# Linear attention and FFN on one core: x's turn ahead of the reciprocal, x1's turn behind it, and a new order of the transfers

## The reference

```
q, k, v = heads(x @ Wq.T + bq), heads(x @ Wk.T + bk), heads(x @ Wv.T + bv)
q, k = exp(q), exp(k)
kv  = cumsum(k[..., :, None] * v[..., None, :], axis=1)     # over the sequence
k1  = cumsum(k, axis=1)
num = einsum('zsD,zsDd->zsd', q, kv)
den = sum(q * k1, axis=-1)
x = layernorm(x + merge(num / den) @ Wo.T + bo)
h = x @ weight @ aux_weight1 @ aux_weight2
x = layernorm(x + tanh(h + bias))
```

## Time and profile before

| | |
|---|---|
| median of 3 runs | 2467.8 us (2459.77 to 2468.61) |
| profiled execution, its own time | 2467.03 us |
| span of its trace | 2465.3 us |
| PE busy | 2321.6 us, 94% |
| DVE busy | 1797.8 us, 73% |
| POOL busy | 1314.3 us, 53% |
| ACT busy | 1052.8 us, 43% |
| mean granted TensorE clock | 0.992 of full speed |

### The profile page before, as it was taken

How to read it: one execution, slowest core, us unless ns; L and a number is a source line. 1 busy time by engine, 2 the same in 40 slices (tenths; PEclk the granted TensorE clock), 3 DMA queues, 4 the chain that set the end, 5 groups by cost and what they waited for, 6 DMA issues and landing times.

```text
span 2465.3 us, 58596 instructions
## 1 busy us (share of the span) xinstructions
PE 2321.6 (94%) x21040; PEld 1907.9 (77%) x21040; DVE 1797.8 (73%) x2710; ACT 1052.8 (43%) x2039; POOL 1314.3 (53%) x1669
## 2 busy tenths in 40 slices
PE   6999999999999999999999999999999999999985
PEld 5778878877877887777777877777777877777764
DVE  4677777777777777777777777777777777777664
ACT  3434444444444444444444444444444444444431
POOL 1455555555655555555555555554555555555553
PEclk9999999999999999999999999999999999999998
DMA  6233333333333333333333333333333333333211
GB/s 162 71 98 103 106 99 102 103 98 96 105 100 100 103 100 97 104 98 99 102 97 100 102 99 100 102 99 99 99 101 100 100 102 99 98 103 96 64 65 52
DMA packets 293918, 241.90 MB, mean 98 GB/s; under 512 B 32848, under 2 KB 225360, under 8 KB 293712
## 3 DMA queue, kind: packets, MB, share of 16 engines
q1 hardware_dynamic: 293712, 238.69, 30.9%
HBM read 139.99 MB, written 98.57 MB: 97 GB/s over the span
## 4 chain that ended last, share of the span: by engine, by line
PE 93%; issue 4%; DVE 1%; ACT 1%; DMA 0%; SPq 0%; POOL 0%; POOLq 0%; ACTq 0%; DVEq 0%
PE G L310 25%; PE G L312 24%; PE G L311 24%; PE SC L377 6%; PE G L389 5%; PE G L364 4%; PE G L410 2%; PE G L401 1%; PE G L411 1%; PE SC L310 0%; PE SC L312 0%; PE SC L311 0%; DMA QT<-wqT 0%; DVE o L656 0%; SPq L272 0%
## 5 line engine op out<-in xcount | busy, mean ns | idle before, releaser
L775 POOL TENSOR_TENSOR qk1L<-WK,qk1H 128x512 fp32r<-128x512 f32 x128 | 165.4, 1292 | 814.7 <-ACT qk1H L555 814.7
L679 DVE RECIPROCAL o<-G 128x512 f32<-128x512 f32 x128 | 424.9, 3320 | 2.8 <-PE G L411 1.4
L673 DVE STREAM_TRANSPOSE SC<-WK 128x512 f32<-128x512 f32 x128 | 93.0, 727 | 448.5 <-DMA WK<-x_rows 448.5
L753 POOL TENSOR_SCALAR_AFFINE_SELECT A<-A 128x512 f32<-128x512 f32 x512 | 314.4, 639 | 10.7 <-issue 6.6
L517 ACT ACTIVATE A<-SC 128x512 f32<-128x512 f32 x512 | 275.3, 591 | 61.1 <-PE G L389 59.7
L792 POOL TENSOR_TENSOR xTL<-xin,xTH 128x512 fp32r<-128x512 f32 x128 | 164.8, 1288 | 245.6 <-ACT xTH L568 245.5
L310 PE MATMUL G<-WfH,x1H 128*128 128x512 f32 x512 | 211.1, 412 | 83.4 <-issue 71.7
L555 ACT ACTIVATE qk1H<-WK 128x512 fp32r<-128x512 f32 x128 | 81.0, 633 | 469.6 <-DVE WK L707 469.6
L724 DVE TENSOR_SCALAR WK<-xres,mv,rstd 128x512 f32<-128x512 f32 x128 | 200.5, 1566 | 86.4 <-POOL rstd L782 86.4
L533 ACT ACTIVATE x1H<-SC 128x512 fp32r<-128x512 f32 x128 | 76.6, 599 | 374.0 <-DVE SC L673 374.0
L310 PE MATMUL G<-xTH,WqH 128*128 128x512 f32 x512 | 203.0, 396 | 28.7 <-POOL xTL L792 21.1
(11 more groups left out here) (107 smaller groups left out, 5597.2 us busy)
## 6 DMA issues: line engine op xcount, KB each, us to landing
xin<-x SPq DMA_DIRECT2D x512, 64.0 KB, 1.9
xres<-x SPq DMA_DIRECT2D x128, 256.0 KB, 3.3
x_rows<-WK SPq DMA_DIRECT2D x128, 256.0 KB, 2.1
WK<-x_rows SPq DMA_DIRECT2D x512, 64.0 KB, 2.0
out<-WK SPq DMA_DIRECT2D x128, 256.0 KB, 2.1
k_rows<-WK SPq DMA_DIRECT2D x120, 256.0 KB, 2.3
WK<-k_rows SPq DMA_DIRECT2D x480, 64.0 KB, 2.0
QT<-wqT SPq DMA_DIRECT2D x4, 256.0 KB, 4.2
```

The costliest lines, as they stand in the source:

```text
L679: nc.vector.reciprocal(oflat, den_ps[:, :]).then_inc(recip_ready, 1)
L753: last = nc.gpsimd.affine_select(out=A[:, j, :, :], in_=A[:, j, :, :], compare_op=ALU.is_ge, fill=0.0, base=0, pattern=[[0, NK], [1, P]], ...
L775: nc.gpsimd.tensor_tensor(qk1L[:, :], WK[:, 7, :], qk1H[:, :].bitcast(F32), ALU.subtract).then_inc(qk1l_ready, 1)
```

## The change

VectorE: x's turn of tile k+8 moves from behind L724 to behind K's turn; the reciprocal follows it; x1's turn moves behind the reciprocal; the finished tile moves ahead of x1L. Queue: K's store and reads move ahead of the store of the finished tile; the load of the residual moves behind x1's reads and gets a wait for x1_ready, which is met by then. No operation and no transfer is added or taken away.

```diff
 queue, slot(c, k):
-                if c.exists(k - 3):
-                    n = k - 3
-                    wait_before(sp, (out_ready, c.count(n + 1)))
-                    sp.dma_start(out_t[n % B, c.it + n // B], y[:, n % 2, :]).then_inc(out_stored[n % B], 16)
                 if c.updates_state(k):
                     wait_before(sp, (k_turned, c.count(k + 1)))
                     sp.dma_start(k_rows, KS).then_inc(k_stored[k % B], 16)
...
+                if c.exists(k - 3):
+                    n = k - 3
+                    wait_before(sp, (out_ready, c.count(n + 1)))
+                    sp.dma_start(out_t[n % B, c.it + n // B], y[:, n % 2, :]).then_inc(out_stored[n % B], 16)
                 n = k - 1
                 if c.exists(n):
                     wait_before(sp, (x1_ready, c.count(k)))
                     sp.dma_start(x1_rows, x1[:, n % 2, :]).then_inc(x1_stored[n % B], 16)
-                if c.exists(k + 1):
...
-                    m = k + 1
-                    sp.dma_start(xres[:, m % 2, :], x_t[m % B, c.it + m // B]).then_inc(xres_loaded[m % B], 16)
                 if c.exists(n):
                     wait_before(sp, (x1_stored[n % B], c.dma_count(n)), (x1_turned, c.count(n)))
...
+                if c.exists(k + 1):
...
+                    wait_before(sp, (x1_ready, c.count(k)))
+                    m = k + 1
+                    sp.dma_start(xres[:, m % 2, :], x_t[m % B, c.it + m // B]).then_inc(xres_loaded[m % B], 16)

 VectorE, slot(c, k), behind K's turn:
-                if ffn:
-                    (x1's turn: wait for x1s_loaded and scores_out[0], transpose into x1T_ps)
+                if c.exists(k + 8):
+                    m = k + 8
+                    wait(dve, xin_loaded[m % B], c.part_count(m))
+                    xblocks = xin[:, m % XIN, :]
+                    nc.vector.transpose(xblocks, xblocks).then_inc(x_turned, 1)
                 if att:
                     (the reciprocal, unchanged)
                 if ffn:
-                    (x1L)
+                    (x1's turn)
                 if fin:
                     (the finished tile, unchanged)
+                if ffn:
+                    (x1L)
...
-                if c.exists(k + 8):
-                    (x's turn, behind L724)
```

More of the change, by code:

```diff
@@ L288, in slot @@
                     sp.dma_start(x1_rows, x1[:, n % 2, :]).then_inc(x1_stored[n % B], 16)
-                if c.exists(k + 1):
-                    if c.static() and c.it * B + k == -1:
-                        sp.wait_ge(c_done, 1)
-                    m = k + 1
-                    sp.dma_start(xres[:, m % 2, :], x_t[m % B, c.it + m // B]).then_inc(xres_loaded[m % B], 16)
                 if c.exists(n):
@@ L298, in slot @@
                                      x1_blocks[j]).then_inc(x1s_loaded[n % B], 16)
+                if c.exists(k + 1):
+                    if c.static() and c.it * B + k == -1:
+                        sp.wait_ge(c_done, 1)
+                    wait_before(sp, (x1_ready, c.count(k)))
+                    m = k + 1
+                    sp.dma_start(xres[:, m % 2, :], x_t[m % B, c.it + m // B]).then_inc(xres_loaded[m % B], 16)
             run_slots(sp, slot, 8, 3, {-7: load_wq_and_biases, -5: load_wk, -4: load_ffn_weights_and_wv,
@@ L667, in slot @@
                                         ).then_inc(k_turned, 1)
+                if c.exists(k + 8):
[3 more added lines that the diff above has]
+                    nc.vector.transpose(xblocks, xblocks).then_inc(x_turned, 1)
+                if att:
+                    wait(dve, den_done, c.count(k + 1))
+                    wait(dve, oh_ready, c.count(k))
+                    wait(dve, ol_ready, c.count(k))
+                    nc.vector.reciprocal(oflat, den_ps[:, :]).then_inc(recip_ready, 1)
                 if ffn:
@@ L674, in slot @@
                                         x1s[:, :].rearrange("p (t g f) -> p g t f", t=HG, f=HD)).then_inc(x1_turned, 1)
[L675 to L679, removed]
+                if fin:
+                    wait(dve, rstd2_ready, c.count(k - 2))
+                    nc.vector.tensor_scalar(yf, yf, mv2[:, 0:1], rstd[:, 1:2],
+                                            ALU.subtract, ALU.mult).then_inc(out_ready, 1)
                 if ffn:
@@ L684, in slot @@
                                             ALU.subtract).then_inc(x1l_ready, 1)
[L685 to L688, removed]
                 n = k + 1
```

## The result

The changed kernel takes 2907.8 us (median of 4 runs, 2901.0 to 2909.8) against 2464.6 for the kernel before: ratio 1.179, 95% interval [1.176, 1.183]. It is 443 us slower. The forecast was 2827, with a range of 2630 to 2960. One of the five executions of e3 took 4612.6 us and is left out of its figures.

A forecast was written before the change was run, and what follows sets the result against it. The prediction took x1's ring (18.51 us a slot) to bound the kernel, just above TensorE's 17.9. A new ring through x's load makes the slot 21.65: 2467 + 370 - 10 = 2827 us, range 2630 to 2960.

The forecast's parts named there:

- the ring of x1: x1's store, reads, turn and VectorE's operations to L724, once per slot: 18.51 us before, 14.5 us alone after the change.
- costs nothing: The reciprocal (3.24 us), ahead of x1's turn, fits VectorE's 4.27 us of idleness, so is free for x1's ring.
- The ring through x's load: New ring: VectorE awaits x's load, queued behind x1's store and reads, which await L724; 22.15 us a slot.
- Its queue part: From L724's end to x's turn: first x load issued after 4.81 us, 9.2 in all, bounds 8.09 and 10.8.
- Its VectorE part: VectorE from x's turn to L724's end: 0.70 + 3.24 + 9.01 = 12.95 us a slot.
- The term that was too small: The slot was forecast at 21.65 us, with no term for VectorE waiting on ScalarE's exponential of K.
- The tail: Last eight slots, no x awaited and reciprocal off x1's ring: between 0 and -23 us, -10 taken.
- the start: The kernel's first slots, which have no x1 ring: 0 us.
- The rule on the shared ports: VectorE's L724 beside GpSimd's L786: first issuer holds the ports, L724 takes 0.55 us; the forecast kept the row's 1.61.
- The rule on the clock: An idle TensorE is throttled; by the page the clock would fall in each slot with the idle stretch.
- The rival built on it: FFN product at 1.2 GHz in every slot and L724 long: 23.0 us a slot, +529, 2986 us; chance 0.08.
- The rival of the other side: x's load lands in time, slot falls to TensorE's 17.9 us below 4.9 us: 2386 us; chance 0.03.

The follow-up runs named there:

- e3: The kernel before with only the queue's new order, VectorE as before: 2447.2 us, ratio 0.992 to before.
- e7: The kernel before with VectorE's new order but x's turn not moved, and the queue as before: 2442.5 us, ratio 0.992.
- e5: The changed kernel with x's load early in the queue and ScalarE's exponential of K ahead of its four state copies: 2351.4 us, ratio 0.953 to before.
- e1: The changed kernel with x's turn put back behind L724, all else as changed: 2442.5 us, ratio 0.990 to before.
- e2: The kernel before with only x's turn moved, ahead of x1's turn and the reciprocal; queue as before: 2736.9 us, ratio 1.110.
- e4: The changed kernel with x's load moved in the queue ahead of the previous slot's x1 store, VectorE as changed: 2368.1 us, ratio 0.960 to before.
- e9: The changed kernel with x's load issued later, behind K's store and reads: 3494.7 us, 587 more than the changed kernel.
- e6: The changed kernel with ScalarE's exponential of K ahead of its four state copies: 2874.7 us, 33 us less than the changed kernel.
- e13: The changed kernel with 12 added matmuls of constants ahead of the FFN product, result unread: 2906.3 us, ratio 1.180 to before.

## Why the prediction was right

**The bound now** was read rightly in kind. Of two limits close together the ring of x1 decides: taking the reciprocal off it (e7) gave 0.8%, and with the waits for transfers off VectorE's way (e5) TensorE has hardly any idle time left. Two sizes were off. TensorE's own work is 17.6 us a slot (e5), not the 17.9 got by taking its idle time from the slot, so the limits stood 0.9 us apart. And the reciprocal's move alone was to win the 0.6 us of idle a slot; e7 won 0.17 (18.34 against 18.51), because the reciprocal, now early, waits for oL, 226.6 us in 112 slots. The prediction's "costs nothing" had left that wait out.

**The ring through x's load** was the mechanism. e1, e2, e4 and e9 tell it apart from everything else in the change: taken away two ways the loss is gone (2442.5, 2368.1), alone it makes 2736.9, and made longer by 5.56 us it makes each slot 4.97 longer.

**Its queue part** was forecast as 4.81 us to the first x load and 9.2 to x's turn. The sum came true (9.23 on the mean), but there is luck in it, since its two parts were off by half a microsecond each way. The trip shown has 4.75 us to the first x load; the mean over the slots is 5.35 (4.5 to 7.5), 0.54 more than forecast. The sum had been made of one undisturbed trip, and in the mean x1's store to its first read is 2.29 us instead of 2.16, the four reads 1.97 instead of 1.74, and the residual's load to x's 0.80 instead of 0.60, because now and then one issue takes over 1 us. The kernel before would have told: there the same transfers, in another order, take 5.35 us on the mean too. From the first x load to x's turn it is then 3.88 us, where 9.2 less 4.81 had left 4.39.

**Its VectorE part** was 12.95, with -0.5 for L724's operation. A slot in which nothing is waited for but rstd and L730 is long has 12.91 us (0.63 + 3.25 + 1.34 + 0.61 + 7.08), and L730 takes 1.08 us on the mean against 1.61, since it is long in one slot and short in the next: both are borne out. The waits below raise it again: 12.91 - 0.53 + 0.43 + 0.52 - 0.33 = 13.0, and 12.98 is measured.

**The term that was too small** is what I put at nothing: the slot is 21.65 + 0.56. 0.43 of it is VectorE's wait for ScalarE's exponential of K. At every fourth slot the scans begin a new group of four tiles and need the KT that ScalarE has just made; with x1's turn moved back behind the reciprocal, ScalarE's x1H, the exponential of Q, the four copies and the exponential of K all come later against VectorE, and the scans wait 1.7 us. I had followed x1H and stopped there. It is 50.4 us, and e6 got 33 back. It comes with VectorE's new order: e1 and e7 have it too (44.4 and 48.7 us, 28 slots each, from 160 to 2200 us), and the kernel before and e2 do not. The rest, 0.13, is about the FFN's lateness (61.0 us, 0.52 a slot) less what the wait for rstd gives back (79.9 us before, 41.4 after, 0.33 a slot).

**The tail** was to give 10 us and gave 2.4, and the start cost 3.4 where I had 0. With the 433 of the slots against 370 this is the 74 us between 2827 and the profiled execution's 2901.0.

**The rule on the shared ports.** I went by the row (1.61 us) against "Who interferes with whom" of the Trainium skill's SBUF — State Buffer. The trace after agrees with the row. L787, GpSimd's addition, never starts ahead of L730 there. In 64 of the 128 slots it starts 0.05 to 0.07 us behind it, and L730 takes 1.6 us. In the other 64 it starts 0.19 us or more behind it, in all but three after L730's end, and L730 takes 0.55. The page's rule, that the first to issue has the ports, fits those three and not the 64. Why it does not hold at so small a distance no run here shows.

**The rule on the clock.** The Trainium skill, TensorE: Matmul & The Clock Gate, "What's actually happening", has the idle array throttled. The trace agrees that the clock falls while TensorE stands still (0.50 from 1311 us on), but not that it would in each such slot: the FFN product met the lower clock in 61 of 117. The rival built on it, 2986, did not come, since the FFN's lateness freed L730. e13 shows that the two about cancel, and so does e9, where the FFN product met the lower clock in all 117 slots and the piece from x's turn to the end of L730 was still 12.9 us.

**The rival of the other side** needed x's load within 5.6 us of L724's end. Nothing in this queue's order allows it; e4 allows it by moving the load, and gives 2368.1, near that rival's 2386.

## What to carry to other kernels

Before an operation is moved ahead in an engine's stream, ask when its input is issued, and what stands ahead of that in the queue: a wait that was free at the end of a slot puts everything behind it on the queue's ring. Take the price of a piece of queue from its mean over many slots, not from one undisturbed trip. Move the load with its consumer: here the same VectorE order costs 18% with the load in its old place and wins 4% with the load one wait earlier. Where an operation's result goes to another engine, follow that engine's stream to the end of the slot, also for the slots that come only every fourth time.

## What was unexpected of the hardware

A fall of TensorE's clock to 1.2 GHz, met by the FFN product in 61 of 117 slots (mean clock 0.931), cost this kernel nothing on balance: 2907.8 us with it, 2906.3 with the product slowed in 26 slots only. VectorE waited longer for the FFN in those slots, and its next operation was shorter by about as much. A single transfer's issue at times takes over 1 us instead of 0.32 to 0.43 (four x loads in 2.44 us instead of 1.84), and the same was seen with the residual's load out of the way (e3), so that what draws it out stays open.
